# Three PSUM tiles for the one-bank loops, and a layer norm split between two adds: a sandwich layer on eight cores

## The chip, the cores and the metric

One Trainium2 chip, the program on 8 cores, each with 1024 of the 8192 token rows. The metric is the device time in microseconds of the slowest core. In this document TensorE, VectorE, ScalarE, GpSimd and SyncE are called by these names, or PE, DVE, ACT, POOL and SP where the profile's rows say so.

## What is computed

```python
x = L0_attn_u                                  # [1, 8192, 4096] fp32
x = x + layernorm(attn(layernorm(x)))
x = x + layernorm(ffn(layernorm(x)))
# attn: K = ifft(c*(k00 - k01*k10/(1+k11))).real   with k_ij sums over 64 states of v/(g - Lambda)
#       y = causal convolution of each row with K (4096 taps) + D*u
# ffn:  x @ kernel + bias + LoRA of the batch (one-hot gate over 16) + shared LoRA, rank 32 each
# layernorm: (x - mean)/sqrt(var + 1e-5), no weights
```

## The kernel before

The program keeps one list of instructions per engine, in the order in which the Python code emits them; there is no scheduler. `E` emits an instruction that raises its engine's counter, `W` puts waits for such counters in front of what follows, `DMA` issues a transfer with a counter of its own. On VectorE and ScalarE, `E` also waits for the instruction before it on the same engine. Each engine, and SP's and POOL's transfer issues, run strictly in that order.

Stage 1 makes the kernel K and the constants. For each of 4096 frequencies and 64 states a grid value is needed: three loops do this in chunks of 512 columns. The loop at L360 (16 chunks, 8 of the real part into xb0, 8 of the imaginary part into xb1) loads a 2 KB row of constants into one of two one-row buffers wh_s (L354, on SP; from the third chunk on it waits for the matmul of two chunks before), spreads it over 64 partitions with an fp32 matmul against ones64s (1 row by 64 columns, L360) into the PSUM tile putil, and ScalarE evacuates it with a scale (L365). Then VectorE and ScalarE work on the grid (L372 to L387: subtract, square, add, Ln, Exp, multiply). The loop at L395 (8 chunks) makes the imaginary part anew in the same way (evacuation L400), L405 and L406 finish it. The loop at L415 (16 chunks) sums over the states with an fp32 matmul (64 rows by 8 columns vmat) into putil, and VectorE copies 8 rows to ya (L419). GpSimd then stores ya to k_scr (L423), and a chain of small steps, transfers and a 64x64 Fourier transform ends in the band matrix tband; after it come the LoRA sums.

All three loops write putil, so the matmul of a chunk waits for the evacuation of the chunk before:

```python
toks = [t_wh, t_stepb, t_bpb]
if prev_sc is not None:
    toks.append(prev_sc)
W("tensor", toks)
```

Stage 2 runs over eight tiles of 128 token rows, in two alternating buffers xb: load u (L678), sums for the layer norm on VectorE (L682) and ScalarE (L686), ln_finalize (L643 to L654: mean, variance, reciprocal, the root on ScalarE at L652, and nbias = -mean*rstd at L654), normalise to bf16 n1b (L690), 32 transposes (L707, copied out by L711), the convolution as 144 matmuls with the banded matrix in eight groups over three PSUM tiles pconv (L726), each group combined with D*n1b into ya by VectorE (L730) and squared for its sum by ScalarE (L735). Then the layer norm of ya: sums (L742, L746), ln_finalize, ScalarE normalises ya in place (L751), VectorE adds it to xb (L754). The result x1 goes to DRAM (L757), behind it on SP the next tile's u load. The statistics of x1 (L761, L765), its layer norm (L769), transposes (L778, copied by L782) and the LoRA-A matmuls (L789) end the tile.

Stage 3 is the feed-forward product: eight blocks of 512 output columns, in each 8 bias matmuls with two rows (L824), 32 x 8 matmuls (L836) with weights loaded on GpSimd's queue (L831), 8 LoRA matmuls (L842); VectorE moves each PSUM tile to fstage (L853), ScalarE squares it (L857), SP stores it to f_scr (L861). In the last block, stage 4 follows for each tile: load x1 and f (L870, L872), finalise, normalise f on ScalarE (L884), add both (L887) and store y (L889).

## Time and profile before

| what | us |
|---|---|
| timed runs, median (lowest, highest) | 1855.12 (1854.48, 1855.75) |
| the profiled execution's own time | 1857.85 |
| its span, slowest core (core 7) | 1856.3 |
| spans of the eight cores | 1822.1 to 1856.3 |
| busy in the span: PE, DVE, ACT, POOL | 950.9, 424.2, 318.5, 167.4 |

The span runs from the first to the last instruction of the slowest core. Busy time is what an engine's instructions took; PEld is TensorE's weight load, which lies beside its matmuls. A row of the time line gives start, duration, engine, line, operation, output and inputs, and in brackets how long the engine had stood idle and which instruction ended the wait. An fp32 matmul appears as two records. The granted clock (PEclk) is a share of full speed: 1.00 is 2.4 GHz, 0.50 is 1.2 GHz.

### The profile page before, as it was taken

The numbers are of one execution on the slowest core, as the hardware profiler recorded it, in microseconds if no ns is written. First come the engines' busy times: TensorE is split into PE (matmuls) and PEld (weight loads), VectorE is DVE, ScalarE is ACT, GpSimd is POOL, SyncE is SP. The second block draws the span as 40 slices with busy tenths as digits, with TensorE's granted clock in tenths as the row PEclk, the third lists the DMA queues.
The fourth block names the chain that finished last, engine by engine and source line by source line (L and its number), as shares of the span: only waits on it lengthen the run. The fifth ranks groups of instructions, "written<-read, shape, count | busy, mean of one in ns | idle before, by whom it ended". The sixth has DMA issues, their size and how long they took to land.

```text
span 1856.3 us, 13068 instructions; the slowest of 8 cores (1822.1 to 1856.3 us)
## 1 busy us (share of the span) xinstructions
PE 950.9 (51%) x4229; PEld 421.7 (23%) x4229; DVE 424.2 (23%) x762; ACT 318.5 (17%) x386; POOL 167.4 (9%) x313
## 2 busy tenths in 40 slices
PE   4353000044738183645647399999899999500000
PEld 0000000022323132222323243343343343200000
DVE  1221254123342424233333301101101101021212
ACT  1410000023131413232232201101101101011211
POOL 0002101100000000000000022222232231100000
PEclk9999999997768585858677698998899898855555
DMA  0000345422020202022020145655566555556464
GB/s 7 1 1 11 66 68 79 85 57 91 1 90 1 91 1 91 12 80 58 33 91 1 45 60 102 111 69 102 102 75 104 102 72 99 133 192 232 187 237 186
DMA packets 66579, 149.79 MB, mean 81 GB/s; under 512 B 16727, under 2 KB 50056, under 8 KB 60576
## 3 DMA queue, kind: packets, MB, share of 16 engines
q0 software_dynamic: 41248, 45.82, 18.8%
q1 hardware_dynamic: 25266, 103.14, 16.0%
q8 instruction: 35, 0.57, 0.1%
q14 instruction: 30, 0.25, 0.1%
HBM read 137.08 MB, written 52.23 MB: 102 GB/s over the span
## 4 chain that ended last, share of the span: by engine, by line
PE 48%; DMA 17%; DVE 16%; ACT 9%; issue 6%; DVEq 1%; SPq 1%; POOL 1%; ACTq 0%; POOLq 0%
PE pffn L836 24%; PE pconv L726 14%; DMA xb<-f_scr 6%; DMA f_scr<-fstage 4%; DVE trv L761 2%; DVE trv L682 2%; DVE xb L754 2%; DVE ya L887 2%; PE ptrb L778 2%; DMA trv<-lora_a 2%; PE putil L360 2%; ACT n1b L690 2%; ACT n1b L769 2%; ACT ya L751 2%; ACT xb L884 2%
## 5 line engine op out<-in xcount | busy, mean ns | idle before, releaser
L836 PE MATMUL pffn<-wbuf,n2fm 128*128 128x512 bf16 x2048 | 463.7, 391 | 4.4 <-DMA wbuf<-wk 4.4
L726 PE MATMUL pconv<-tband,xfmt 128*128 128x512 bf16 x1152 | 265.7, 395 | 8.1 <-DVE xfmt L711 8.1
L836 PEld LDWEIGHTS pffn<-wbuf,n2fm 128*128 128x128 bf16 x2048 | 204.2, 100 | 263.5 <-issue 35.8
L831 POOL DMA_DIRECT2D wbuf<-wk x256 | 135.1, 529 | 1093.9 <-PE pffn L836 1081.0
L853 DVE TENSOR_SCALAR_CACHE_REDUCE fstage<-pffn 128x512 f32<-128x512 f32 x64 | 44.3, 691 | 498.1 <-PE pffn L842 481.8
L726 PEld LDWEIGHTS pconv<-tband,xfmt 128*128 128x128 bf16 x1152 | 115.9, 101 | 156.1 <-issue 31.1
L857 ACT ACTIVATE tra<-fstage 128x512 bf16<-128x512 f32 x64 | 40.3, 629 | 550.3 <-DVE fstage L853 545.8
L778 PE MATMUL ptrb<-idsb,n1b 128*128 128x128 bf16 x256 | 32.9, 310 | 195.5 <-ACT n1b L769 195.5
L707 PE MATMUL ptrb<-idsb,n1b 128*128 128x128 bf16 x256 | 29.8, 308 | 190.7 <-ACT n1b L690 189.0
L730 DVE SCALAR_TENSOR_TENSOR ya<-n1b,dbc,pconv 128x512 f32<-128x512 bf16 x64 | 47.8, 747 | 226.0 <-PE pconv L726 226.0
L735 ACT ACTIVATE tra<-ya 128x512 bf16<-128x512 f32 x64 | 40.3, 629 | 275.6 <-DVE ya L730 275.6
L887 DVE TENSOR_TENSOR ya<-xb 128x4096 f32<-128x4096 f32 x8 | 35.4, 4425 | 174.3 <-ACT xb L884 174.3
L778 PEld LDWEIGHTS ptrb<-idsb,n1b 128*128 128x128 bf16 x256 | 24.7, 140 | 203.3 <-issue 203.3
L707 PEld LDWEIGHTS ptrb<-idsb,n1b 128*128 128x128 bf16 x256 | 25.5, 141 | 194.8 <-issue 194.2
L884 ACT ACTIVATE xb<-xb,stf_nbias,stf_rstd 128x4096 f32<-128x4096 f32 x8 | 30.4, 3799 | 144.6 <-DMA xb<-f_scr 144.6
L789 PE MATMUL pax<-n2fm,astkT 128*64 128x128 bf16 x256 | 33.0, 310 | 32.4 <-DVE n2fm L782 32.4
L782 DVE COPY n2fm<-ptrb 128x1024 bf16<-128x1024 bf16 x32 | 22.1, 691 | 98.8 <-PE ptrb L778 98.8
L824 PE MATMUL pffn<-bhl,ones2bs 2*128 2x512 bf16 x64 | 30.6, 501 | 26.2 <-DVE fstage L853 24.5
L686 ACT ACTIVATE tra<-xb 128x4096 bf16<-128x4096 f32 x8 | 28.9, 3617 | 84.4 <-DMA xb<-u 84.4
L754 DVE TENSOR_TENSOR xb<-xb,ya 128x4096 f32<-128x4096 f32 x8 | 35.4, 4425 | 33.0 <-ACT ya L751 33.0
L415 PE MATMUL putil<-xb,vmat 64*8 64x512 f32 x32 | 29.8, 1031 | 24.9 <-DVE ya L419 16.8
L682 DVE TENSOR_SCALAR_CACHE_REDUCE trv<-xb 128x4096 bf16<-128x4096 f32 x8 | 35.4, 4419 | 17.5 <-DMA xb<-u 16.7
(208 smaller groups left out, 562.6 us busy)
## 6 DMA issues: line engine op xcount, KB each, us to landing
wbuf<-wk POOLq DMA_DIRECT2D x256, 128.0 KB, 3.2
xb<-u SPq DMA_DIRECT2D x8, 2048.0 KB, 14.4
x_scr<-xb SPq DMA_DIRECT2D x8, 2048.0 KB, 9.2
f_scr<-fstage SPq DMA_DIRECT2D x64, 256.0 KB, 3.0
xb<-x_scr SPq DMA_DIRECT2D x8, 2048.0 KB, 9.3
xb<-f_scr SPq DMA_DIRECT2D x8, 2048.0 KB, 13.8
y<-ya SPq DMA_DIRECT2D x8, 2048.0 KB, 7.5
n1b<-lora_b POOLq DMA_DIRECT2D x16, 256.0 KB, 3.9
```

The costliest lines, as they stand in the source:

```text
L682: t_rs = E("vector", lambda v, xbt=xbt: v.tensor_scalar(out=trv[:, :], in0=xbt[:, :], scalar1=1.0, scalar2=None, op0=OP.mult, op1=OP.add, ...
L707: tlast = E("tensor", lambda t, c=c, r=r, j=j: t.transpose(out=ptrb[r % 2][:, 128 * j:128 * j + 128], in_=n1b[:, 128 * c:128 * c + 128], i ...
L726: tg = E("tensor", lambda t, g=g, ij=ij, j0=j0: t.matmul(out=pconv[g % 3][:, :], lhsT=xfmt[:, 128 * ij:128 * ij + 128], rhs=tband[:, j0:j0 ...
L730: conv_ev[g] = E("vector", lambda v, g=g: v.scalar_tensor_tensor(out=ya[:, 512 * g:512 * g + 512], in0=n1b[:, 512 * g:512 * g + 512], scal ...
L735: E("scalar", lambda s, g=g: s.activation(out=tra[:, 512 * g:512 * g + 512], in_=ya[:, 512 * g:512 * g + 512], func=AF.Square, accum_out=y ...
L754: t_x1 = E("vector", lambda v, xbt=xbt: v.tensor_tensor(out=xbt[:, :], in0=xbt[:, :], in1=ya[:, :], op=OP.add))
L778: tlast = E("tensor", lambda t, c=c, r=r, j=j: t.transpose(out=ptrb[r % 2][:, 128 * j:128 * j + 128], in_=n1b[:, 128 * c:128 * c + 128], i ...
L831: t_wload[kg] = DMA("gpsimd", f"wload{kg % 4}", lambda g, f=f, oc=oc, kg=kg: g.dma_start(out=wbuf[kg % 4][:, :], in_=wk[128 * f:128 * f + ...
L836: tlast = E("tensor", lambda t, f=f, t2=t2, kg=kg: t.matmul(out=pffn[t2][:, :], lhsT=bass.AP(n2fm, TOK * f + P * t2, [[FC * TOK, P], [1, P]]),
L853: t_fev[(oc, t2)] = E("vector", lambda v, t2=t2, oc=oc, sbuf_i=sbuf_i: v.tensor_scalar(out=fstage[sbuf_i][:, :], in0=pffn[t2][:, :], scala ...
L884: t_lnf = E("scalar", lambda s: s.activation(out=xb[1][:, :], in_=xb[1][:, :], func=AF.Identity, bias=stf["nbias"][:, :], scale=stf["rstd" ...
L887: t_add = E("vector", lambda v: v.tensor_tensor(out=ya[:, :], in0=xb[0][:, :], in1=xb[1][:, :], op=OP.add))
```

## The change

Three edits in the first stage, one in the tiles and the tail. The three loops write in turn to putil, pconv0 and pconv1 (a list called pot), and the first convolution gets waits for the last evacuations. In the loops at L360 and L415 a matmul waits for the evacuation of three chunks before. In the loop at L395 a matmul waits for the one of three chunks before and, except in the first chunk, for that of the chunk before as well. In the tiles, ScalarE's normalisation (L751) goes; VectorE copies the row's nbias to a column of a new tile nall and computes x1 without it, as ya*rstd + xb in one scalar_tensor_tensor. The statistics of x1 and its layer norm don't change when a constant is taken from a row. The missing nbias is added in the tail, where L887 becomes a scalar_tensor_tensor as well.

```diff
@@ -249,6 +249,7 @@
...
+        nall = e(nc.sbuf_tensor("nall", [P, 8], F32))
@@ -345,6 +346,7 @@
         prev_sc = None
+        pot = [putil, pconv[0], pconv[1]]
         kwh = 0
         for half, dst in [(0, xb[0]), (1, xb[1])]:
             for cchunk in range(8):
@@ -354,16 +356,16 @@
                 t_wh = DMA("sync", f"wh{kwh % 2}", lambda s, src_c=src_c, cchunk=cchunk, kwh=kwh: s.dma_start(
                     out=wh_s[kwh % 2][:, :], in_=src_c[0:1, 512 * cchunk:512 * cchunk + 512]))
                 toks = [t_wh, t_stepb, t_bpb]
-                if prev_sc is not None:
-                    toks.append(prev_sc)
+                if kwh >= 3:
+                    toks.append(gb_toks[kwh - 3])
                 W("tensor", toks)
                 tmm = E("tensor", lambda t, kwh=kwh: t.matmul(
-                    out=putil[0:NS, :], lhsT=ones64s[:, :],
+                    out=pot[kwh % 3][0:NS, :], lhsT=ones64s[:, :],
                     rhs=wh_s[kwh % 2][:, :], start=True, stop=True))
                 gb_mms.append(tmm)
                 W("scalar", [tmm])
-                prev_sc = E("scalar", lambda s, dst=dst, cchunk=cchunk: s.activation(
-                    out=dst[0:NS, 512 * cchunk:512 * cchunk + 512], in_=putil[0:NS, :],
+                prev_sc = E("scalar", lambda s, dst=dst, cchunk=cchunk, kwh=kwh: s.activation(
+                    out=dst[0:NS, 512 * cchunk:512 * cchunk + 512], in_=pot[kwh % 3][0:NS, :],
                     func=AF.Identity, scale=stepb[:, :]))
                 gb_toks.append(prev_sc)
                 kwh += 1
@@ -391,33 +393,40 @@
                 W("sync", [gb_mms[kwh - 2]])
             t_wh = DMA("sync", f"wh{kwh % 2}", lambda s, cchunk=cchunk, kwh=kwh: s.dma_start(
                 out=wh_s[kwh % 2][:, :], in_=cin["whim"][0:1, 512 * cchunk:512 * cchunk + 512]))
-            W("tensor", [t_wh, prev_sc2])
+            W("tensor", [t_wh, gb_toks[kwh - 3], t_s12 if cchunk == 0 else prev_sc2])
             tmm = E("tensor", lambda t, kwh=kwh: t.matmul(
-                out=putil[0:NS, :], lhsT=ones64s[:, :],
+                out=pot[kwh % 3][0:NS, :], lhsT=ones64s[:, :],
                 rhs=wh_s[kwh % 2][:, :], start=True, stop=True))
             gb_mms.append(tmm)
             W("scalar", [tmm])
-            prev_sc2 = E("scalar", lambda s, cchunk=cchunk: s.activation(
-                out=xb[1][0:NS, 512 * cchunk:512 * cchunk + 512], in_=putil[0:NS, :],
+            prev_sc2 = E("scalar", lambda s, cchunk=cchunk, kwh=kwh: s.activation(
+                out=xb[1][0:NS, 512 * cchunk:512 * cchunk + 512], in_=pot[kwh % 3][0:NS, :],
                 func=AF.Identity, scale=stepb[:, :]))
+            gb_toks.append(prev_sc2)
             kwh += 1
...
         prev_ev = None
+        ks_evs = []
+        kk = 0
         for src, outrow, tok in [(xb[0], 0, t_rdre), (xb[1], 32, t_rdim)]:
             for cchunk in range(8):
                 toks = [tok, t_rec, t_rdim]
-                if prev_ev is not None:
-                    toks.append(prev_ev)
+                if kk >= 3:
+                    toks.append(ks_evs[kk - 3])
+                else:
+                    toks.append(gb_toks[-1])
                 W("tensor", toks)
-                tmm = E("tensor", lambda t, src=src, cchunk=cchunk: t.matmul(
-                    out=putil[0:8, :], lhsT=vmat[:, :], rhs=src[0:NS, 512 * cchunk:512 * cchunk + 512],
+                tmm = E("tensor", lambda t, src=src, cchunk=cchunk, kk=kk: t.matmul(
+                    out=pot[kk % 3][0:8, :], lhsT=vmat[:, :], rhs=src[0:NS, 512 * cchunk:512 * cchunk + 512],
                     start=True, stop=True))
                 W("vector", [tmm])
-                prev_ev = E("vector", lambda v, outrow=outrow, cchunk=cchunk: v.tensor_copy(
-                    out=ya[outrow:outrow + 8, 512 * cchunk:512 * cchunk + 512], in_=putil[0:8, :]))
+                prev_ev = E("vector", lambda v, outrow=outrow, cchunk=cchunk, kk=kk: v.tensor_copy(
+                    out=ya[outrow:outrow + 8, 512 * cchunk:512 * cchunk + 512], in_=pot[kk % 3][0:8, :]))
+                ks_evs.append(prev_ev)
+                kk += 1
@@ -719,6 +728,8 @@
                     toks.append(conv_ev[g - 3])
                 elif last_convevac is not None:
                     toks.append(last_convevac)
+                elif t_i == 0:
+                    toks += [t_ksum_done, gb_toks[-1]]
@@ -747,12 +758,11 @@
             t_ra, t_nba = ln_finalize(sta, D, t_ys, t_yq)
-            W("scalar", [t_nba])
-            t_lnya = E("scalar", lambda s: s.activation(
-                out=ya[:, :], in_=ya[:, :], func=AF.Identity, bias=sta["nbias"][:, :], scale=sta["rstd"][:, :]))
-            W("vector", [t_lnya])
-            t_x1 = E("vector", lambda v, xbt=xbt: v.tensor_tensor(
-                out=xbt[:, :], in0=xbt[:, :], in1=ya[:, :], op=OP.add))
+            W("vector", [t_ra, t_nba])
+            t_nsv = E("vector", lambda v, t_i=t_i: v.tensor_copy(out=nall[:, t_i:t_i + 1], in_=sta["nbias"][:, :]))
+            t_x1 = E("vector", lambda v, xbt=xbt: v.scalar_tensor_tensor(
+                out=xbt[:, :], in0=ya[:, :], scalar=sta["rstd"][:, :], op0=OP.mult,
+                in1=xbt[:, :], op1=OP.add))
@@ -884,7 +894,9 @@
                     t_lnf = E("scalar", lambda s: s.activation(
                         out=xb[1][:, :], in_=xb[1][:, :], func=AF.Identity, bias=stf["nbias"][:, :], scale=stf["rstd"][:, :]))
                     W("vector", [t_lnf, t_x1l] + ([t_yst[t_i - 1]] if t_i >= 1 else []))
-                    t_add = E("vector", lambda v: v.tensor_tensor(out=ya[:, :], in0=xb[0][:, :], in1=xb[1][:, :], op=OP.add))
+                    t_add = E("vector", lambda v, t_i=t_i: v.scalar_tensor_tensor(
+                        out=ya[:, :], in0=xb[0][:, :], scalar=nall[:, t_i:t_i + 1], op0=OP.add,
+                        in1=xb[1][:, :], op1=OP.add))
```

TensorE's order in the loop at L360 (L362 in the changed kernel), from the first chunk on. wh_s0 and wh_s1 are the two buffers of constants, dma_wh0 and dma_wh1 their loads, tok_scalar is ScalarE's counter, by which a matmul waits for an evacuation. Before:

```order
L360 MATMUL putil<-wh_s0,ones64s 64x512 [waits dma_wh0,tok_vector]
L360 MATMUL putil<-wh_s1,ones64s 64x512 [waits dma_wh1,tok_vector,tok_scalar]
L360 MATMUL putil<-wh_s0,ones64s 64x512 [waits dma_wh0,tok_vector,tok_scalar]
L360 MATMUL putil<-wh_s1,ones64s 64x512 [waits dma_wh1,tok_vector,tok_scalar]
L360 MATMUL putil<-wh_s0,ones64s 64x512 [waits dma_wh0,tok_vector,tok_scalar]
```

The same place now:

```order
L362 MATMUL putil<-wh_s0,ones64s 64x512 [waits dma_wh0,tok_vector]
L362 MATMUL pconv0<-wh_s1,ones64s 64x512 [waits dma_wh1,tok_vector]
L362 MATMUL pconv1<-wh_s0,ones64s 64x512 [waits dma_wh0,tok_vector]
L362 MATMUL putil<-wh_s1,ones64s 64x512 [waits dma_wh1,tok_vector,tok_scalar]
L362 MATMUL pconv0<-wh_s0,ones64s 64x512 [waits dma_wh0,tok_vector,tok_scalar]
L362 MATMUL pconv1<-wh_s1,ones64s 64x512 [waits dma_wh1,tok_vector,tok_scalar]
```

The number and order of the matmuls are the same; the output rotates, and tok_scalar is waited for from the fourth chunk on, with a value three evacuations old. The buffers of constants still alternate between two.

TensorE in the loop at L395 (L397 in the changed kernel), its last chunks and the start of the loop at L415. Before:

```order
L395 MATMUL putil<-wh_s0,ones64s 64x512 [waits dma_wh0,tok_vector]
L395 MATMUL putil<-wh_s1,ones64s 64x512 [waits dma_wh1,tok_scalar]
L395 MATMUL putil<-wh_s0,ones64s 64x512 [waits dma_wh0,tok_scalar]
...
L415 MATMUL putil<-xb0,vmat 8x512 [waits tok_vector,tok_scalar] x8
L415 MATMUL putil<-xb1,vmat 8x512 [waits tok_vector,tok_scalar] x8
```

Now:

```order
L397 MATMUL pconv0<-wh_s0,ones64s 64x512 [waits dma_wh0,tok_scalar,tok_vector]
L397 MATMUL pconv1<-wh_s1,ones64s 64x512 [waits dma_wh1,tok_scalar]
L397 MATMUL putil<-wh_s0,ones64s 64x512 [waits dma_wh0,tok_scalar]
...
L422 MATMUL putil<-xb0,vmat 8x512 [waits tok_vector,tok_scalar]
L422 MATMUL pconv0<-xb0,vmat 8x512 [waits tok_vector,tok_scalar]
L422 MATMUL pconv1<-xb0,vmat 8x512 [waits tok_vector,tok_scalar]
```

The outputs rotate in both loops. At L397 the value of tok_scalar is that of the chunk before, from the second chunk on; at L422 the value of tok_vector is that of three chunks before.

VectorE behind the convolution of a tile, where trv and the sta tiles are small (columns of sums, mean, variance, rstd and nbias) and xb is the tile of the residual. Before:

```order
L650 RECIPROCAL sta_rstd<-sta_var 128x1
L654 TENSOR_SCALAR sta_nbias<-sta_mean,sta_rstd 128x1
L754 TENSOR_TENSOR xb<-xb,ya 128x4096
L761 TENSOR_SCALAR trv,st_s<-xb 128x4096
```

Now:

```order
L659 RECIPROCAL sta_rstd<-sta_var 128x1
L663 TENSOR_SCALAR sta_nbias<-sta_mean,sta_rstd 128x1
L762 COPY nall<-sta_nbias 128x1
L763 SCALAR_TENSOR_TENSOR xb<-ya,sta_rstd,xb 128x4096
L771 TENSOR_SCALAR trv,st_s<-xb 128x4096
```

VectorE has one small copy more, and its add reads ya unnormalised. On ScalarE, L751 stood between L652 (the root) and L765 (the squares of x1) and is gone.

## Rows read from the trace of the kernel before

**Rows 1.** The page's chain that ended last, shares of the span by engine

```profile
PE 48%; DMA 17%; DVE 16%; ACT 9%; issue 6%; DVEq 1%; SPq 1%; POOL 1%; ACTq 0%; POOLq 0%
```

**Rows 2.** Windows: from:to, length, busy of PE, PEld, DVE, ACT, POOL, clock, DMA, GB/s

```profile
20.70:67.40 46.70, 30.95 (x32) 4.51 (x32) 4.48 (x28) 10.91 (x16) 0.00 (x0) 1.00 0.00 1
...
118.20:165.70 47.50, 29.77 (x32) 1.89 (x32) 10.87 (x16) 0.00 (x0) 0.00 (x0) 1.00 0.00 0
```

**Rows 3.** Time line of the loop at L360: first chunk, a load issue, last chunk

```profile
20.70 1.94 PE L360 MATMUL putil<-wh_s,ones64s 1*64 1x512 f32 x2 [0.54 <-DVE bpb L318]
...
63.50 41.14 SPq L392 DMA_DIRECT2D wh_s<-whim  x8
...
64.41 1.94 PE L360 MATMUL putil<-wh_s,ones64s 1*64 1x512 f32 x2 [0.98 <-ACT xb L365]
```

**Rows 4.** The loops at L395 and L415: time line, last pair in the chain, single records

```profile
89.89 0.68 ACT L400 ACTIVATE xb<-putil,stepb 64x512 f32<-64x512 f32 x1
...
118.26 1.86 PE L415 MATMUL putil<-xb,vmat 64*8 64x512 f32 x2 [8.13 <-DVE xb L406]
120.30 0.68 DVE L419 COPY ya<-putil 8x512 f32<-8x512 f32 x1 [2.29 <-PE putil L415]
...
162.97 1.88 PE putil L415 x2
...
L360 PE MATMUL putil<-wh_s,ones64s x32: 1056/1068/1082, 20.7 to 65.3; 1*64 1x512 f32 x32
...
  POOL k_scr L423: 165.6, 1
```

**Rows 5.** Window behind the wh_s issue at 63.50; the store of 1 KB; issues

```profile
64.30:64.45 0.15, 0.04 (x1) 0.07 (x2) 0.00 (x0) 0.00 (x0) 0.00 (x0) 1.00 0.04 14
...
211.80 1.58 DMA krev_scr<-tband
...
f_scr<-fstage SPq DMA_DIRECT2D x64, 256.0 KB, 3.0
```

**Rows 6.** Time line behind the first tile's convolution

```profile
436.84 0.21 DVE L654 TENSOR_SCALAR sta_nbias<-sta_mean,sta_rstd 128x1 f32<-128x1 f32 x1 [0.53 <-ACT sta_rstd L652]
437.21 3.80 ACT L751 ACTIVATE ya<-ya,sta_nbias,sta_rstd 128x4096 f32<-128x4096 f32 x1 [0.54 <-DVE sta_nbias L654]
441.18 4.42 DVE L754 TENSOR_TENSOR xb<-xb,ya 128x4096 f32<-128x4096 f32 x1 [4.12 <-ACT ya L751]
...
461.00 3.62 ACT L686 ACTIVATE tra<-xb 128x4096 bf16<-128x4096 f32 x1 [4.38 <-DMA xb<-u]
...
467.91 4.42 DVE L682 TENSOR_SCALAR_CACHE_REDUCE trv<-xb 128x4096 bf16<-128x4096 f32 x1
```

**Rows 7.** Groups: the two-input forms of VectorE (busy, mean ns, idle before)

```profile
L555 DVE SCALAR_TENSOR_TENSOR ya<-trv,gq_s,ya 128x4096 f32<-128x4096 bf16 x2 | 9.0, 4484 | 7.3 <-DMA trv<-lora_a 7.3
...
L406 DVE SCALAR_TENSOR_TENSOR xb<-xb,ya 64x4096 f32<-64x4096 f32 x1 | 4.4, 4417 | 0.1
```

**Rows 8.** Clock: windows (columns as in rows 2), and transposes under either clock

```profile
401.20:484.30 83.10, 43.01 (x240) 23.54 (x241) 28.35 (x51) 25.21 (x26) 0.00 (x0) 0.72 0.17 51
...
569.64:654.83 85.19, 45.22 (x240) 24.10 (x241) 28.36 (x51) 25.21 (x26) 0.00 (x0) 0.70 0.16 50
...
401.20:432.40 31.20, 31.20 (x144) 13.97 (x144) 5.29 (x14) 5.06 (x14) 0.00 (x0) 1.00 0.00 1
484.30:488.70 4.40, 4.40 (x11) 1.58 (x12) 0.75 (x2) 0.72 (x2) 0.00 (x0) 0.50 0.01 4
...
1067.80:1071.20 3.40, 3.40 (x8) 0.95 (x8) 0.00 (x0) 0.00 (x0) 0.00 (x0) 0.50 0.00 0
...
1071.30:1075.80 4.50, 4.50 (x12) 1.60 (x12) 0.00 (x0) 0.00 (x0) 0.36 (x1) 0.50 0.01 4
...
395.94 1.87 PE L707 MATMUL ptrb<-idsb,n1b 128*128 128x128 bf16 x16 [116.38 <-ACT n1b L690]
...
479.40 1.86 PE L707 MATMUL ptrb<-idsb,n1b 128*128 128x128 bf16 x16 [10.44 <-ACT n1b L690]
```

## The prediction

> **What bounds the kernel now.** I read the page's busy shares first, then the chain of waits, then the time line of the three places that the edits touch. TensorE is busy 51% of the span, so no single engine is the bound; the chain that ended last is a mixture of matmuls (48%), transfers, VectorE, ScalarE and hand-over time [rows 1]. Nearly everything outside the dense matmul stages is one serial chain in which exactly one engine works. A microsecond cut from a link of that chain comes off the span, as long as nothing else is late right behind it.
>
> The program has four stages: the state-space kernel and the constants (0 to 370 us, serial), eight token tiles (370 to 1067.8), the feed-forward matmuls (to 1605) and the tail of eight layer norms (to 1856.3). The edits sit in the first stage, in the tiles, and with one instruction per tile in the tail.
>
> In the first stage 46.7 and 47.5 us go to the loops at L360 and L415 over 512-column chunks [rows 2]; the loop at L395 is half as long and of the same pattern. A pair of fp32 matmul records takes 1.94 us [rows 3], the evacuation 0.68 [rows 4], and the next pair waits for it, because all chunks use one PSUM tile. The period is (64.41-20.70)/15 = 2.914 us at L360, of which 0.29 are two hand-overs of 0.15, and (162.97-118.26)/15 = 2.981 us at L415 [rows 3, 4].
>
> In a tile, the layer norm behind the convolution runs on the path: bias ready, ScalarE normalises ya (L751, 3.80 us), VectorE adds (L754, 4.42 us), and only then do the statistics and the next tile's work follow [rows 6].
>
> **The change part by part.**
>
> *Loop at L360, 16 chunks, three PSUM tiles.* A matmul now waits for the evacuation three chunks back, which is long done. Late next is one of two things. (a) TensorE itself: the pair takes 1.94 us, of which the last record accounts for 1.07 [rows 4], so the second record starts 0.87 after the first and pairs that follow each other without a wait take 2 x 0.87 = 1.74 us. (b) The row of constants in wh_s, of which there are still two buffers: SP issues a buffer's next load when the matmul that read it has ended. One buffer's cycle is: pair 1.94, end to issue 0.07 (the first L392 issue stands at 63.50, the pair before it began one period ahead of 64.41, at 61.50, and so ended at 63.43 [rows 3]), the landing, and 0.2 from the landing through the waits to the matmul; two chunks are served per cycle. The landing of wh_s has no row in the list of issues. Its bytes moved 0.8 to 0.95 us after the issue [rows 5], so it can't be under 1.0. The nearest row is the 1 KB store krev_scr<-tband, 1.58 us with an issue of 0.50 where SP's takes 0.22: 1.3. The largest of SP's rows that could stand for it is f_scr<-fstage with 3.0 us for 256 KB [rows 5]. I take 1.4, close to the nearest row. The cycle is 1.94+0.07+1.4+0.2 = 3.61, so 1.805 us per chunk, just above (a). Saved: 15 x (2.914-1.805) = 16.6 us. Bounds: 15 x (2.914-1.74) = 17.6 with the engine as the limit; with 3.0 us the cycle is 5.21, 2.605 a chunk, and 4.6 us are saved.
>
> The Trainium skill (DMA: Bandwidth & Descriptors, Anatomy of one DMA) gives a fixed cost of about 2.0 us per transfer, mostly the confirmation after the last byte. By it the cycle would be 4.21, 2.105 a chunk, and this loop would save 12.1 us; no row here shows a 2 KB load's landing, and the 1.58 of the store is below the page's figure.
>
> *Loop at L395, 8 chunks.* The new wait list still holds prev_sc2, the evacuation of the chunk before (for all but the first). The tiles rotate, the serial chain stays: matmul, evacuation, matmul. The order's rows say so too: the waits of rows 2 to 8 of that loop are dma_wh and tok_scalar, as before. The first matmul waits for nothing new, and its evacuation stands behind Ln and Exp until 89.89 [rows 4]. Gain 0; bounds 0 to 7 x 1.1 = 7.8 if I misread it.
>
> *Loop at L415, 16 chunks.* No transfer is in this loop. The pair takes 1.86 there [rows 4]; in the ratio of 1.74 to 1.94 that is 1.67 back to back, and since the columns are the same 512 as at L360 I take 1.72, nearer to 1.74. VectorE needs 0.68 per copy plus some 0.2 of hand-over, so TensorE is the limit. Saved 15 x (2.981-1.72) = 18.9 us. Bounds: if each pair must have left the array before the next starts, 1.86+0.15 = 2.01 a chunk and 14.6; the upper bound is in the first rival.
>
> What follows both loops (the subtraction at L372, the store of k_scr on POOL) waits for the last evacuation alone and moves forward in full; POOL stood idle for 165.6 us until that store [rows 4]. A conv bank as scratch costs nothing: the first convolution comes at 401.2 [rows 8].
>
> *Tile: the normalisation.* Before, the bias (L654) starts at 436.84 and ends at 437.05; ScalarE starts at 437.21; the add starts at 441.18 [rows 6]. After, on VectorE alone: gap 0.17, a copy of one column into nall (0.15, as the other one-column rows), gap 0.17, and scalar_tensor_tensor starts at 437.54. It takes what the add took, if that form is no slower: with two fp32 inputs at 64 partitions the row of L406 has 4.417 against 4.416 for tensor_tensor at L387, and at 128 partitions L555 with a bf16 input has 4.48 [rows 7]. I take 4.42; bounds 4.42 to 4.48, which is 0.5 us over eight tiles. Saved 441.18-437.54 = 3.64 a tile, 29.1 for eight. What is late next moves along: x1's store and the next u load are issued behind the add, and u lands at 461.0, when VectorE is busy with this tile's transposes until 467.8 [rows 6]. So a u load that starts earlier by the same 3.64 has the same 6.9 us of slack.
>
> *What the clock gives and takes.* The period of tiles 2 to 7 is 85.2 to 85.4 us (tile 3 with 85.19 stands in [rows 8] for the six), that of tile 1 is 83.10. In tile 1 the whole convolution runs at the granted 1.00 (2.4 GHz); in tile 2 its first 4.4 us run at 0.50 (1.2 GHz) and the rest at 1.00 [rows 8]. TensorE had stood idle for 10.44 us before that tile's transposes. The half clock costs 85.3-83.1 = 2.2 us a tile. Where the rise falls against a convolution that comes earlier isn't to be read from before. I take it 0.5 us later, 0.27 us of cost for seven tiles, -1.9. Bounds: the clock already up, as in tile 1, +15.4; the rise as late as at the start of the feed-forward part, where the first matmul starts at 1067.8 and the rows up to 1075.8 have 0.50 [rows 8], some 8.1 us against 4.6 here: (8.1-4.6)/2 = 1.75 a tile, -12.3.
>
> *Tail.* L887 becomes scalar_tensor_tensor with a column of nall: same two fp32 tiles, same 4.42 [rows 7]. Gain 0, bound +0.06 x 8 = 0.5 us of loss. The loads, the layer norm and y's store aren't touched.
>
> Sum: 16.6 + 0 + 18.9 + 29.1 - 1.9 + 0 = 62.7 us. Against the profiled execution, 1857.85 - 62.7 = 1795.15. That execution is 2.73 us above the median of the timed runs (1855.12), so the forecast for the median is 1792.4 us, 3.4% faster.
>
> **The rivals.**
>
> 1. *TensorE's clock rises in the front loops.* The page writes 1.00 for them, but that is no grant: 16 transposes at 395.94, under the same 1.00, take 1.87 us, and those at 479.40, under 0.50, take 1.86 [rows 8]. So before 400 us the matmuls ran at 1.2 GHz. With the gaps gone TensorE is busy 96% (1.74 of 1.805) instead of 66% (30.95 of 46.70 [rows 2]) of the loop, and may get 2.4. Then a pair takes 1.09 and the L360 cycle is 2.76, 1.38 a chunk: 6.4 us more; at L415 VectorE's copy with its hand-over, about 0.95 a chunk, is the limit: 15 x 0.77 = 11.6 more. Time: 1792.4 - 18.0 = 1774.4. Against it: the eight two-row matmuls at 1067.8 fill 3.40 of 3.40 us and stay at 0.50 [rows 8], and these here use one row, or eight columns. The Trainium skill (TensorE: Matmul & The Clock Gate, What's actually happening) says that the clock is half by default and that sustained busy time releases it; by it this rival would hold. The two-row matmuls speak against it. Chance 10%.
>
> 2. *The constants set the pace.* Landing at 3.0, or two loads in flight that delay each other: 2.605 a chunk, 12.0 less. Time 1804.4. For it: two buffers only, and only 0.065 us a chunk between my cycle and the engine. Against it: one 2 KB packet on an idle queue. Chance 9%.
>
> 3. *The clock takes the tile's gain.* The -12.3 above instead of -1.9: 1802.8. For it: all six later periods agree within 0.2 us, which looks like a cycle that the clock helps to set. Chance 10%.
>
> 4. *Matmuls don't overlap across the waits.* Each pair must end first: at L360 2.09 a chunk (4.3 less), at L415 2.01 (4.3 less): 1801.0. Against it: 144 convolution matmuls in 31.24 us [rows 8], eight groups with waits between them, no gap. Chance 6%.
>
> 5. *The fused form is dear (slower than before).* Both big adds, L754 and L887, become scalar_tensor_tensor with a per-row scalar. If that form ran at half the rate at 128 partitions with two fp32 tiles, 16 x 4.42 = 70.8 us come on top: 1863.2, slower. It decides from 62.7/16 = 3.9 us per instruction, that is from 8.3 us each. L406 shows the form at 4.417 with 64 partitions, so this is nearly excluded. Chance 1%.
>
> **How the numbers follow.** My forecast holds 64%, with 1784 to 1800 as its own range. To 8 in 10, with the first rival below and the next three above it: 1777 to 1806. A change of 2% is about what a measurement of this kernel can tell from none; that limit lies at 1818.0. It is passed only if two of the rivals 2 to 4 come together with a misread term, or with the fifth. Faster by over 2%: 0.95; within: 0.04; slower: 0.01.
>
> **What would show it.** Matmul starts 1.8 us apart at L360, 2.91 apart at L395, 1.72 at L415; the first subtraction at about 50.8 instead of 67.4; no ScalarE pass between the bias and the add in the tiles, and the add 0.5 us behind the bias' end; period of the tiles 81.5 to 82.2; the big adds 4.42 both; the tail the same length from the last matmul. Wrong if the L395 loop shrinks, if fp32 records fall below 0.6 us, if the granted clock comes up before the convolution or much later than 5 us into it, or if any of the big adds takes over 4.5.

## The result and the profile after

The changed kernel takes 1790.68 us (median of 11 runs, 1783.43 to 1837.73), the kernel before 1854.44 (10 runs). The ratio is 0.9659, with a 95% interval of 0.964 to 0.9678: faster by 63 us (63.2 by the ratio, 63.8 by the medians). Forecast were 1792.4 us and a ratio of 0.966. The longest execution of the changed kernel (1837.73) is one in which the cores of one die showed a lower granted clock than the others, and it doesn't count in the ratio.

The profiled execution after is a short one (1783.43 us) and its slowest core is core 1, not core 7. For a comparison by stage I take core 1 in both profiles:

| event on core 1 | before, us | after, us | gained so far |
|---|---|---|---|
| first matmul of the first loop (L360, L362) | 21.36 | 21.40 | 0 |
| first subtraction (L372, L374) | 68.07 | 52.30 | 15.8 |
| store of k_scr (L423, L432) | 166.97 | 132.10 | 34.9 |
| first convolution starts | 396.05 | 363.73 | 32.3 |
| eighth convolution starts | 993.30 | 930.49 | 62.8 |
| feed-forward part starts (L824, L834) | 1065.05 | 998.66 | 66.4 |
| last matmul group (L842, L852) starts | 1597.17 | 1531.14 | 66.0 |
| end | 1850.6 | 1781.4 | 69.2 |

So the gain of the front loops outlives the long chain of transfers behind them, and the feed-forward part is the same length. The 2.6 us that core 1 seems to lose on the way (34.9 to 32.3) are the scatter of one core: in the mean of the eight cores 34.8 us are gained at the store, 35.3 at the first convolution, 63.7 at the eighth and 67.2 at the feed-forward part. In the tail the two executions differ by 3 us on core 1. A single core's tail takes from 233 to 258 us in the kept profiles, and from 233 to 253 in the kernel before alone, so a gain of a few microseconds shows in the windows of a stage and not in the end of one execution.

The time line of the first loop and of the tile in the changed kernel (core 1), to be set beside [rows 3] and [rows 6]:

```profile
21.40 1.93 PE L362 MATMUL putil<-wh_s,ones64s 1*64 1x512 f32 x2 [0.54 <-DVE bpb L319]
23.14 3.77 PE L362 MATMUL pconv<-wh_s,ones64s 1*64 1x512 f32 x4
...
49.28 1.93 PE L362 MATMUL putil<-wh_s,ones64s 1*64 1x512 f32 x2
...
51.37 0.68 ACT L367 ACTIVATE xb<-putil,stepb 64x512 f32<-64x512 f32 x1 [1.12 <-PE putil L362]
52.30 2.35 DVE L374 TENSOR_SCALAR xb<-xb,lam_s 64x4096 f32<-64x4096 f32 x1 [22.37 <-ACT xb L367]
...
401.63 0.21 DVE L663 TENSOR_SCALAR sta_nbias<-sta_mean,sta_rstd 128x1 f32<-128x1 f32 x1 [0.53 <-ACT sta_rstd L661]
402.01 0.15 DVE L762 COPY nall<-sta_nbias 128x1 f32<-128x1 f32 x1 [0.17 <-DVE sta_nbias L663]
402.27 4.48 DVE L763 SCALAR_TENSOR_TENSOR xb<-ya,sta_rstd,xb 128x4096 f32<-128x4096 f32 x1
```

The sixteenth pair of L362 starts 27.88 us after the first: (49.28-21.40)/15 = 1.859 us a chunk. The add of the tile starts 0.43 us behind the bias' end; before it was 4.13 (441.18-437.05 in [rows 6]). The next fence has the windows of the three loops, with the columns of [rows 2]:

```profile
21.40:51.20 29.80, 29.60 (x32) 4.66 (x32) 4.50 (x28) 10.23 (x15) 0.00 (x0) 1.00 0.01 1
67.10:95.90 28.80, 15.48 (x16) 2.27 (x16) 4.48 (x2) 12.78 (x10) 0.00 (x0) 1.00 0.00 1
103.10:130.80 27.70, 27.46 (x32) 3.98 (x32) 10.20 (x16) 0.00 (x0) 0.00 (x0) 1.00 0.00 1
```

TensorE is now busy 99% of the first and the third loop (66% and 63% in [rows 2]). The loop in the middle has its old length, and its old waits:

```profile
75.61 1.93 PE L397 MATMUL pconv<-wh_s,ones64s 1*64 1x512 f32 x2 [6.51 <-ACT xb L402]
77.69 0.68 ACT L402 ACTIVATE xb<-pconv,stepb 64x512 f32<-64x512 f32 x1 [2.23 <-PE pconv L397]
78.49 0.28 PEld L397 LDWEIGHTS putil<-wh_s,ones64s 1*64 1x64 f32 x2 [2.63 <-issue]
78.52 1.94 PE L397 MATMUL putil<-wh_s,ones64s 1*64 1x512 f32 x2 [0.98 <-ACT xb L402]
```

The 0.98 us of idling until "ACT xb L402" is the wait on the evacuation of the chunk before: rotating tiles doesn't help while it stands.

The groups of the fused adds, and three of the tiles of the changed kernel (one window per tile, from one convolution's start to the next):

```profile
L897 DVE SCALAR_TENSOR_TENSOR ya<-xb,nall 128x4096 f32<-128x4096 f32 x8 | 35.9, 4484 | 170.4 <-ACT xb L894 170.4
...
L763 DVE SCALAR_TENSOR_TENSOR xb<-ya,sta_rstd,xb 128x4096 f32<-128x4096 f32 x8 | 35.9, 4484 | 0.8
```

```profile
445.50:527.23 81.73, 44.95 (x241) 23.84 (x242) 28.56 (x52) 21.40 (x25) 0.00 (x0) 0.72 0.13 52
527.23:606.69 79.46, 43.01 (x240) 23.54 (x241) 28.57 (x52) 21.41 (x25) 0.00 (x0) 0.72 0.14 53
606.69:688.12 81.43, 44.97 (x241) 24.08 (x241) 28.57 (x52) 21.41 (x25) 0.00 (x0) 0.71 0.14 52
```

ScalarE has lost 3.8 us a tile (25.21 in [rows 8], 21.41 here). The tile that takes 79.46 has 1.94 us less of TensorE: its convolution ran wholly at 2.4 GHz.

### The profile page after: what moved, and what is told of

Its sections match the earlier page's. It is cut to its first block, busy times and chain, and to the rows that moved or that the text cites. A ratio compares the mean times of both kernels' runs of the same rounds, so it can differ in the third digit from the quotient of the medians.

```text
span 1781.4 us, 13070 instructions; the slowest of 8 cores (1762.2 to 1781.4 us)
## 1 busy us (share of the span) xinstructions
PE 940.6 (53%) x4229; PEld 422.4 (24%) x4229; DVE 426.4 (24%) x770; ACT 288.1 (16%) x378; POOL 167.4 (9%) x313
## 4 chain that ended last, share of the span: by engine, by line
PE 50%; DMA 17%; DVE 17%; ACT 7%; issue 6%; DVEq 1%; SPq 1%; POOL 1%; ACTq 0%; POOLq 0%
PE pffn L846 25%; PE pconv L737 15%; DMA xb<-f_scr 6%; DMA f_scr<-fstage 5%; DVE xb L763 2%; DVE ya L897 2%; DVE trv L771 2%; DVE trv L691 2%; PE ptrb L788 2%; ACT n1b L779 2%; ACT n1b L699 2%; ACT xb L894 2%; DMA n1b<-lora_b 2%; DMA trv<-lora_a 2%; PE pax L799 1%
## 5 line engine op out<-in xcount | busy, mean ns | idle before, releaser
L737 PE MATMUL pconv<-tband,xfmt 128*128 128x512 bf16 x1152 | 262.7, 392 | 8.8 <-DVE xfmt L720 8.8
L788 PE MATMUL ptrb<-idsb,n1b 128*128 128x128 bf16 x256 | 32.9, 310 | 167.3 <-ACT n1b L779 167.3
L897 DVE SCALAR_TENSOR_TENSOR ya<-xb,nall 128x4096 f32<-128x4096 f32 x8 | 35.9, 4484 | 170.4 <-ACT xb L894 170.4
L834 PE MATMUL pffn<-bhl,ones2bs 2*128 2x512 bf16 x64 | 30.4, 497 | 27.8 <-DVE fstage L863 26.1
L691 DVE TENSOR_SCALAR_CACHE_REDUCE trv<-xb 128x4096 bf16<-128x4096 f32 x8 | 35.4, 4420 | 16.1 <-DMA xb<-u 14.9
L586 PE MATMUL ptrb<-idsb,trv 64*128 64x64 bf16 x32 | 2.3, 234 | 65.8 <-ACT trv L574 63.2
L763 DVE SCALAR_TENSOR_TENSOR xb<-ya,sta_rstd,xb 128x4096 f32<-128x4096 f32 x8 | 35.9, 4484 | 0.8
```

What stands on the lines that cost most here:

```text
L691: t_rs = E("vector", lambda v, xbt=xbt: v.tensor_scalar(out=trv[:, :], in0=xbt[:, :], scalar1=1.0, scalar2=None, op0=OP.mult, op1=OP.add, ...
L737: tg = E("tensor", lambda t, g=g, ij=ij, j0=j0: t.matmul(out=pconv[g % 3][:, :], lhsT=xfmt[:, 128 * ij:128 * ij + 128], rhs=tband[:, j0:j0 ...
L763: t_x1 = E("vector", lambda v, xbt=xbt: v.scalar_tensor_tensor(out=xbt[:, :], in0=ya[:, :], scalar=sta["rstd"][:, :], op0=OP.mult, in1=xbt ...
L788: tlast = E("tensor", lambda t, c=c, r=r, j=j: t.transpose(out=ptrb[r % 2][:, 128 * j:128 * j + 128], in_=n1b[:, 128 * c:128 * c + 128], i ...
L897: t_add = E("vector", lambda v, t_i=t_i: v.scalar_tensor_tensor(out=ya[:, :], in0=xb[0][:, :], scalar=nall[:, t_i:t_i + 1], op0=OP.add, in ...
```

## The experiments

The ratios are to the kernel before, run in the same session; a difference of two ratios times 1854.44 gives what is called microseconds by the ratios. The medians of different sessions can be some 4 us apart for the same kernel (1850.65 and 1854.44 for the kernel before), so where medians and ratios differ, the ratios are the fairer comparison. Each edit is against the changed kernel unless said otherwise.

**Only the three PSUM tiles.** The layer norm of the tiles and the tail's add as before.

```diff
-            W("vector", [t_ra, t_nba])
-            t_nsv = E("vector", ... nall[:, t_i:t_i + 1] ...)
-            t_x1 = E("vector", ... scalar_tensor_tensor ...)
+            W("scalar", [t_nba])
+            t_lnya = E("scalar", ... activation(out=ya, in_=ya, bias, scale) ...)
+            W("vector", [t_lnya])
+            t_x1 = E("vector", ... tensor_tensor ...)
```

> Only the three PSUM tiles; the layer norm of the tiles and the tail's add are as before. Theory (independent terms on one serial chain): the loops give 16 + 19 = 35 us, ratio to before about 0.981, time about 1819 us; tile periods stay at 85.3 us. Rival A (the gain of the loops is lost again in the transfers behind them, and most of the change's 64 us comes from the tiles): under 25 us, above 1829 us. Rival B (the two parts need each other, through the clock): the two parts alone add up to clearly less than 64 us.

Measured: 1815.53 us, ratio 0.9802 (0.9777 to 0.9827), that is 36.7 us; the interval reaches across 2%, so this half alone is not clearly beyond it. Between the first and the eighth convolution lie 596.1 us in the mean of the eight cores, against 596.0 before: the tiles are untouched. The theory holds.

**Only the layer norm.** The kernel before with the other half of the diff.

> Only the layer norm's part; the three loops keep one PSUM tile. Theory: 3.6 us a tile for eight tiles, 29, minus 0.06 us for each of the sixteen fused adds, minus 1 to 3 us that the low clock takes back: 25 to 28 us, ratio about 0.986, about 1828 us; tile period 81.9 us instead of 85.3. Rival (the clock takes most of it back): under 15 us, above 1839 us.

Measured: 1827.25 us, ratio 0.986 (0.9833 to 0.9886), 26.0 us. It is clear of no change, but within 2%. Seven tiles take 568.94 us on its slowest core, 81.3 each, and 566.7 in the mean of the eight, against 567.6 in the changed kernel. Together the halves give 36.7+26.0 = 62.7 us, the whole 63.2. They add up, though the intervals of the two halves leave some 4 to 5 us open on each. Rival A of the first experiment (under 25 us) is out; rival B (the parts need each other) is out but for that margin.

**The loop at L395 set free.**

```diff
-            W("tensor", [t_wh, gb_toks[kwh - 3], t_s12 if cchunk == 0 else prev_sc2])
+            W("tensor", [t_wh, gb_toks[kwh - 3]] + ([t_s12] if cchunk == 0 else []))
```

> The changed kernel, and in the loop at L395 a matmul no longer waits for the evacuation of the chunk before (only for that of three chunks before). Theory (that wait alone keeps this loop at 2.91 us a chunk): three matmuls run ahead beside Ln and Exp, the others follow at 1.85, the last evacuation comes 9 to 10 us earlier; about 1781 us. Rival (this loop is bound by its two buffers of constants or by the evacuations): under 4 us.

Measured: 1776.17 us, ratio 0.9599 (0.9572 to 0.9627); by the ratios 11 us less than the changed kernel. The evacuations, first to last, on core 3:

```profile
74.65 1.46 ACT L402 ACTIVATE xb<-pconv,stepb 64x512 f32<-64x512 f32 x2
76.20 0.68 ACT L402 ACTIVATE xb<-putil,stepb 64x512 f32<-64x512 f32 x1
77.56 0.68 ACT L402 ACTIVATE xb<-pconv,stepb 64x512 f32<-64x512 f32 x1 [0.68 <-PE pconv L397]
...
84.80 0.68 ACT L402 ACTIVATE xb<-pconv,stepb 64x512 f32<-64x512 f32 x1 [1.26 <-PE pconv L397]
```

The first three follow without a wait: their matmuls ran beside Ln and Exp. From first to last it is 10.15 us, against 20.39 (74.78 to 95.17) in the changed kernel. That one wait cost 10.2 us; the store of k_scr comes 10.5 us earlier in the mean of the eight cores.

**Four buffers of constants** (on top of the last edit).

```diff
-        wh_s = [... for i in range(2)]        # and kwh % 2, kwh - 2
+        wh_s = [... for i in range(4)]        # and kwh % 4, kwh - 4
```

> As the one before (e3), with four buffers of constants instead of two. Theory (in the changed kernel the loop at L360 runs at 1.86 us a chunk because a buffer's cycle of matmul, load and waits takes 3.72 us for two chunks, and TensorE alone would take 1.71): L360 falls to 1.71 to 1.74 a chunk, 2 us less than e3; about 1779 us, a difference that only the time line can show. Rival (the pace of 1.86 is TensorE's own with a wait between pairs): L360 stays at 1.86.

Measured: 1774.65 us, ratio 0.9596 (0.9569 to 0.9623), no difference from the last one that the runs can tell. The time line can:

```profile
21.29 1.94 PE L362 MATMUL putil<-wh_s,ones64s 1*64 1x512 f32 x2 [0.54 <-DVE bpb L319]
...
46.91 1.91 PE L362 MATMUL putil<-wh_s,ones64s 1*64 1x512 f32 x2
```

(46.91-21.29)/15 = 1.708 us a chunk, where two buffers gave 1.859 (changed kernel, core 1) and 1.865 (the edit before, core 3). With four it is 1.708 on all eight cores; with two it lies between 1.82 and 1.90, depending on core and run. So the pace of the changed kernel is that of the two buffers, 3.72 us for two chunks, and TensorE's own is 1.71. Of the 3.72, 1.93 are the pair, 0.07 the step to the issue and 0.2 the waits by the prediction's reading; some 1.5 us remain for the landing of 2 KB, an estimate, where I had 1.4. The remainder rests on those readings; no row shows the landing itself.

**One, and three, microseconds more in each tile.** Four, and twelve, more one-column copies of 0.26 us on VectorE between the bias and the big add.

```diff
+            for _k in range(4):        # range(12) in the second
+                E("vector", ... tensor_copy(out=nall[:, t_i:t_i + 1], in_=sta["nbias"]) ...)
```

> The changed kernel with four more one-column copies on VectorE between the bias and the big add of each tile (0.26 us each, 1.04 us a tile, on the path). Theory (the low clock at the start of each convolution gives and takes: work added or taken between two convolutions is partly made up by the time that the convolution runs at 1.2 GHz): the period of the tiles stays at 81.9 within 0.3 us, and under 3 of the 8.3 us show. Rival (the clock's share is the same whatever the convolution's start): the period becomes 82.8 to 83.0, the time goes up by 8 us, to about 1799.

> The changed kernel with twelve more one-column copies in the same place (3.1 us a tile, 25 us for eight). This brings the length of what lies between two convolutions nearly back to that of the kernel before, and by the theory the period goes to 84 to 85.3 us, so that 17 to 27 us are lost and the matmuls of the convolutions that begin at 1.2 GHz take 33.4 us. By the rival the period is 81.8 + 3.1 = 84.9 for all tiles, 25 us lost. The two differ less here than in e6; together with e6 the run says whether the cost is in proportion (8 and 25) or in a step (under 3, then over 17).

Measured: 1797.34 us, ratio 0.9691 (0.9659 to 0.9723), and 1804.75 us, ratio 0.9746 (0.9725 to 0.9768). The windows over seven tiles on core 1, of the changed kernel, then of either:

```profile
363.73:930.49 566.76, 311.04 (x1680) 167.10 (x1681) 199.98 (x364) 149.84 (x175) 0.00 (x0) 0.72 0.14 52
```

```profile
364.19:937.04 572.85, 310.44 (x1680) 167.22 (x1681) 204.41 (x392) 149.83 (x175) 0.00 (x0) 0.71 0.14 52
```

```profile
364.98:949.10 584.12, 306.68 (x1680) 165.78 (x1681) 213.01 (x448) 149.83 (x175) 0.00 (x0) 0.72 0.16 51
```

Of 7 x 1.04 = 7.3 us added, 6.1 show (5.3 in the mean of the eight cores); of 21.8 us, 17.4 (17.5). My theory of the first run fell. It took the changed kernel's period for 81.9 us, where it is 566.76/7 = 80.97; one microsecond more made it 81.84, so 0.87 of the 1.04 us show and not the third that I expected. Three made it 83.45, less than the 84 to 85.3 expected. Of the small addition 1.2 to 2.0 us of 7.3 are made up, of the large one a fifth, not all of the one and little of the other, so there is no step. What makes it up are the convolutions. The seven of the windows take 229.3 us together in the changed kernel, 228.0 with one microsecond more and 225.4 with three (four of the seven run in 31.24). The totals say less: by the medians one microsecond a tile cost 6.7 us of the 8.3 added and three cost 14.1 of 25 (5.9 and 16.1 by the ratios), by the profiled executions (1804.04 and 1783.43) 20.6. The profiled execution of the changed kernel is the shortest of its eleven. That the totals of the larger addition show less than the windows isn't explained.

**128 columns in the stationary tile of the third loop.** The sums over the states are the same; rows 8 to 127 of PSUM get zeros that nobody reads.

```diff
-        vmat = e(nc.sbuf_tensor("vmat", [NS, 8], F32))
+        vmat = e(nc.sbuf_tensor("vmat", [NS, P], F32))     # columns 8 to 127 set to zero
-                    out=pot[kk % 3][0:8, :], lhsT=vmat[:, :], ...
+                    out=pot[kk % 3][:, :], lhsT=vmat[:, :], ...
```

> The changed kernel with the stationary tile of the loop at L415 (L422) padded with zeros from 8 to 128 columns, so that the same 16 pairs of fp32 matmuls of 512 columns write all 128 rows of PSUM; VectorE copies the same 8 rows. Theory (the two-row matmuls and these stay at 1.2 GHz because they use little of the array): the clock may rise here, the records fall from 1.05 to 0.6 us and the chunk from 1.71 to under 1.2 us, 8 us gained. Rival (fp32 pairs with 64 rows of the array don't raise the clock, whatever their columns): 1.71 us a chunk as before, and a weight load that is a little longer, 0 to 3 us lost.

Measured: 1785.96 us, ratio 0.9635 (0.961 to 0.966), an interval that overlaps the changed kernel's; the store of k_scr comes at 131.2 us in the mean of the eight cores, 131.6 in the changed kernel. The row of the loop's records decides:

```profile
L423 PE MATMUL pconv<-xb,vmat x20: 1057/1057/1057, 104.7 to 127.7; 64*128 64x512 f32 x20
```

1.057 us a record (1.054 in the changed kernel), and the starts of the pairs stay about 1.71 us apart (102.85 to 128.58 for fifteen). The theory falls: with every column in use and TensorE without a gap for 27 us, these fp32 pairs on 64 rows stayed at 1.2 GHz. What of them keeps it there (64 rows, fp32, zeros in most of the columns) wasn't separated.

**Constants loaded straight to 64 partitions.** The loops at L360 and L395 go. A third such load, not in the cut below, makes the imaginary part anew where L395 stood.

```diff
-        for half, dst in [(0, xb[0]), (1, xb[1])]:   # load a row, matmul, evacuate, 16 chunks
+        for nm, dst in [("whre", xb[0]), ("whim", xb[1])]:
+            bro[nm] = DMA("sync", ..., dma_start(out=dst[0:NS, :],
+                in_=bass.AP(cin[nm].tensor, 0, [[0, NS], [1, D]])))
+        t_dre = ... tensor_scalar(xb[0], scalar1=stepb, scalar2=lam_s[:, 0:1], op0=mult, op1=subtract)
```

> The changed kernel without the loops at L360 and L395: the rows of constants are loaded from DRAM straight to 64 partitions (1 MB each, three loads), and one tensor_scalar multiplies by the step and subtracts lambda, in place of matmul, evacuation and subtraction. The rest is as in the changed kernel. Theory (these loops are on the chain for every microsecond of theirs, and a 1 MB load takes 5 to 10 us): the first subtraction starts at about 30 us instead of 52, the second about 13 us behind the sum of squares instead of 29; 36 to 40 us gained, about 1752 us. Rival (something else, such as the constants of the products or the loads themselves, is late by nearly as much): under 20 us.

Measured: 1746.41 us, ratio 0.9429 (0.9403 to 0.9455), 44 us less than the changed kernel by the medians, 43 by the ratios.

```profile
14.30 0.47 SPq L349 DMA_DIRECT2D xb<-whre  x1
...
28.83 0.15 DVE L338 TENSOR_TENSOR vmat<-vmat,tmp 64x1 f32<-64x1 f32 x1 [0.17 <-DVE tmp L336]
29.23 2.40 DVE L352 TENSOR_SCALAR xb<-xb,stepb,lam_s 64x4096 f32<-64x4096 f32 x1 [0.25 <-DVE vmat L338]
...
63.25 1.86 PE L389 MATMUL putil<-xb,vmat 64*8 64x512 f32 x2 [43.34 <-DVE xb L375]
```

The 1 MB load takes 8.5 us (its row in the list of issues) and is there long before VectorE is through with the small products (vmat). The loop over the states starts at 63.25 instead of 103.16, 39.9 us earlier; the theory said 36 to 40 us of gain. The store of k_scr comes 39.2 us earlier in the mean of the eight cores.

**Clock up before the convolution.** TensorE idles while ScalarE writes n1b; eight matmuls whose result is overwritten go there.

```diff
+            W("tensor", [t_nb1, t_tband, ...])
+            for _k in range(8):
+                E("tensor", ... matmul(out=pconv[2][:, :], lhsT=tband[:, 0:128],
+                    rhs=tband[:, 512:1024], start=True, stop=True))
```

> The changed kernel with eight idle-time matmuls (128x128 by 128x512, bf16, into a PSUM tile that the convolution overwrites) ahead of each tile's transposes: TensorE runs them while ScalarE writes n1b, where it would stand idle for 3.8 us. Theory (what differs between tiles is only whether the clock is at 1.2 or 2.4 GHz when the convolution begins): all eight convolutions take 31.24 us, against 262.7 us for the eight in the changed kernel's profile, 12 to 13 us gained, about 1778 us, tile period 79.4 to 79.6. Rival A (the gap of 1.0 us between transposes and convolution, or the transposes, let the clock stay low or fall again): under 4 us gained. Rival B (the matmuls run past n1b and hold the transposes up): slower by up to 1 us a tile.

Measured: 1773.95 us, ratio 0.959 (0.9572 to 0.9608), 16.7 us less than the changed kernel by the medians, but 12.8 by the ratios.

```profile
433.22 3.57 PE L704 MATMUL pconv<-tband 128*128 128x512 bf16 x8 [6.33 <-DVE st_nbias L663]
437.33 1.05 PE L721 MATMUL ptrb<-idsb,n1b 128*128 128x128 bf16 x16 [0.54 <-ACT n1b L699]
438.95 0.61 PE L721 MATMUL ptrb<-idsb,n1b 128*128 128x128 bf16 x8 [0.57 <-DVE xfmt L725]
439.74 0.61 PE L721 MATMUL ptrb<-idsb,n1b 128*128 128x128 bf16 x8 [0.19 <-DVE xfmt L725]
441.36 31.24 PE L742 MATMUL pconv<-tband,xfmt 128*128 128x512 bf16 x144 [1.01 <-DVE xfmt L725]
```

```profile
439.00:443.00 4.00, 2.80 (x24) 1.65 (x25) 2.35 (x4) 0.00 (x0) 0.00 (x0) 1.00 0.00 0
```

All eight convolutions of this core take 31.24 us, and 61 of the 64 on the eight cores take no more; the other three take 32.9 to 33.2. Sixteen transposes take 1.05 us instead of 1.87, which I hadn't counted: 0.85 us a tile less in all. Seven tiles take 550.21 us, 16.6 less than in the changed kernel: 229.3 - 7 x 31.24 = 10.6 from the convolutions and 7 x 0.85 = 6.0 from the transposes. In the mean of the eight cores it is 16.4. That the ratios show only 12.8 fits the scatter of the tails (242.2 us in the mean of the changed kernel's profile, 246.5 here), but isn't shown to come from them.

**Both of the last two.**

> The broadcast loads (e9) and the idle-time matmuls (e10) together. If they are independent, 1746 - 12.5 = about 1734 us.

Measured: 1727.38 us, ratio 0.9334 (0.931 to 0.9358). The forecast took 12.5 us for the matmuls. This is the fastest version, 63 us below the changed kernel by the medians and 60 by the ratios. The two parts are nearly independent: the eight cores reach the feed-forward part 57.4 us earlier in the mean, against 40.0 and 18.8 with one part each. The edit that frees L395 is contained in it, since the loop is gone.

## Why the prediction was right, point by point

*L360.* Forecast 1.805 us a chunk and 16.6 us, measured 1.859 and 15.8 at the first subtraction. That two buffers of constants set the pace and not TensorE is shown by the run with four. By the estimate above the landing was taken 0.1 us too short. The fixed cost of 2.0 us that the Trainium skill gives (DMA: Bandwidth & Descriptors, Anatomy of one DMA) is its figure for transfers that GpSimd issues, which the prediction left out, and this load is issued by SyncE. It would have made it 2.105 a chunk; the trace with 1.859 doesn't bear it out for this load.

*L395.* Forecast 0, measured 0: 2.91 us a chunk, and taking out the wait that was named gave 10.2 us in the trace. My upper bound for it (7.8 us) was too small, because three chunks run ahead beside Ln and Exp and I had counted only the pace.

*L415.* Forecast 1.72 us a chunk and 18.9 us, measured (128.71-103.16)/15 = 1.703 and 34.9-15.8 = 19.1 us at the store of k_scr.

*The layer norm.* Forecast 3.64 us a tile. Measured 4.13-0.43 = 3.70 less 0.06 for the longer add, 3.64. The fused form takes 4.484 us at 128 partitions, the upper bound and not the 4.42 that I took from L406; 0.5 us over eight tiles, and as much again in the tail. It isn't the 8.3 us from which the fifth rival decides.

*The clock.* Here the step failed, in sign: -1.9 us forecast. Core for core, the eight convolutions together take 1.3 to 5.4 us less than before, 3.2 in the mean (266.2 to 263.0 us; on core 1 268.1 to 262.7). My step took the clock's rise as a little later for every tile. In fact one or two of the eight convolutions on each core, 13 of 64, met a clock already up (31.24 us on core 1), against 2 of 64 before. That is one of the prediction's own signs of being wrong. On core 1 it rose among the transposes ahead of the third convolution, before which TensorE had been idle for 10.43 us:

```profile
522.39 1.87 PE L716 MATMUL ptrb<-idsb,n1b 128*128 128x128 bf16 x16 [10.43 <-ACT n1b L699]
524.41 1.48 PE L716 MATMUL ptrb<-idsb,n1b 128*128 128x128 bf16 x16 [0.16 <-DVE xfmt L720]
```

The second sixteen took 1.48 us and not 1.87, and the granted clock is 0.50 up to 525.3 and 1.00 from 525.4 on, before the convolution at 527.23. Why this happened in these tiles and not in the others, no run separates. The term lay within its bounds (+15.4 to -12.3), and the third rival's -12.3 didn't come.

*Mechanism and luck.* The two loops and the layer norm came as forecast, each to within 1 us, and by the mechanism that was named. The total is closer than the terms deserve. At the start of the feed-forward part the profiles show 67.2 us gained in the mean of the eight cores, 4.5 more than the forecast sum, nearly all of it the clock's 5.1 us from -1.9 to +3.2. The medians of the timed runs show 63.8. The profiled execution is the shortest of eleven, and where the others spend their few microseconds more, no trace shows. That the median came within 1.7 us of the forecast is in part luck. The stretch from the store of k_scr to the first convolution gave and took nothing: 229.5 us before and 229.0 after in the mean of the cores, between 224 and 235 on single ones.

*The range.* The outer range doesn't follow from the chances: rivals 2 to 4, at 1801.0 to 1804.4, all lie inside 1777 to 1806, so by the list it holds 89% and not 8 in 10.

*The first rival* (clock up in the loops) is out: TensorE is busy 99% there and its fp32 records stay at 1.05 us. The granted 1.00 that the rows of these loops carry was rightly not believed. The changed kernel shows the same once more. This window lies at the start of its first convolution:

```profile
363.80:368.20 4.40, 4.40 (x11) 1.56 (x12) 0.76 (x2) 0.72 (x2) 0.00 (x0) 1.00 0.00 0
```

Eleven matmuls in 4.40 us under a written 1.00, as many as under 0.50 in [rows 8]: no change of the clock had been recorded yet, and TensorE ran at 1.2 GHz.

*The second rival* came a fifteenth of the way (1.859 between 1.805 and 2.605). *The fourth* is out with 1.703 us at L415, since a pair alone takes 1.86.

## What to carry to other kernels

More PSUM tiles help a chain of matmul and evacuation only where every wait on the chunk before is gone, and then the next pair of buffers sets the pace: work its cycle out before promising the engine's. On a serial chain, ask first whether the loop is needed at all; here three loads with a partition step of zero did the work of 24 matmuls and 24 evacuations. And where TensorE idles a known few microseconds ahead of dense work, matmuls that nobody reads can pay: they took 3.6 us of idle time and gave 2.4 us a tile by the windows, 1.6 by the ratios. Compare stage by stage on the same core, or in the mean of all cores: between two cores, or at the end of one execution, a few microseconds are scatter.

## What the runs showed of the hardware that I had not expected

- TensorE stayed at 1.2 GHz through fp32 pairs that kept it 99% busy for 27 to 30 us, with one row or 64, with 8 columns or 128 (1.054 to 1.057 us for most records). It went to 2.4 GHz after eight bf16 matmuls on all 128 rows (3.57 us; the granted clock is 0.50 up to 436.9 and 1.00 from 437.0 on).
- Transposes run faster with the clock up: 16 take 1.05 us instead of 1.87, and they keep it up until the convolution. The Trainium skill (TensorE: Matmul & The Clock Gate, Part 4: PE-mode transpose) says that full clock doesn't engage for them; here the eight matmuls in front had raised it, and the transposes kept it. In the changed kernel it rose with nothing but transposes on TensorE behind 10.43 us of idling (the rows above), so the trace doesn't bear the page out.
- Time added between two convolutions is made up in part by the clock: 1.2 to 2.0 us of 7.3, 4.3 to 4.4 of 21.8 (core 1 and the mean of the cores). So in this kernel a microsecond per tile is worth some 0.7 to 0.85 us of a tile's period until the clock is held up.
- The same 4096-element fp32 form takes 4.484 us at 128 partitions with a scalar column, and 4.417 at 64 partitions with an immediate.
